# Attention scores built on the array's two 64-row halves, and shifted two query groups later

## The reference, cut to what matters

```
qk  = einsum('bhld,bhrd->bhlr', q, k) / sqrt(16)      # content
qk += einsum('bhld,lrd->bhlr', q, rel_emb[r - l + 511]) # rel: a window that depends on l
att = softmax(qk, axis=-1)
out = einsum('bhlr,bhrd->bhld', att, v)
```

## Time and profile before

| | before |
|---|---|
| median of 3 runs | 6504.95 us (6501.69 to 6511.04) |
| the profiled execution | 6501.09 us |
| its span, first to last instruction | 6499.3 us |
| TensorE busy | 6203.9 us, 95% |
| DVE busy | 5036.1 us, 77% |
| ACT, POOL busy | 48%, 56% |
| TensorE matmuls | 178176 |
| granted TensorE clock | 0.99 of full speed |

### The profile page before, as it was taken

The page is one execution under the profiler, slowest core; times in us unless marked ns, Lnnn a source line. Parts: engine busy times, 40 slices in busy tenths (PEclk is TensorE's granted clock), DMA queues, the critical chain, the costliest instruction groups (busy, mean ns, idle before and its releaser), DMA issues.

```text
span 6499.3 us, 408509 instructions
## 1 busy us (share of the span) xinstructions
PE 6203.9 (95%) x178176; PEld 5783.0 (89%) x178176; DVE 5036.1 (77%) x10289; ACT 3134.0 (48%) x5145; POOL 3640.9 (56%) x4707
## 2 busy tenths in 40 slices
PE   5999999999999999999999999999999999999997
PEld 4999899999999999999999999899999999998997
DVE  3777777777787777777777777777777777777776
ACT  2444444444444444444444444444444444444444
POOL 5555555555565555555555555555555555555555
PEclk8999999999999999999999999999999999999998
DMA  3111121111212112121111211112111121211210
GB/s 86 37 44 50 37 58 37 51 45 35 58 36 59 35 35 61 35 60 33 42 56 35 60 36 48 45 39 58 35 52 43 35 58 38 59 35 33 62 35 27
DMA packets 570089, 296.73 MB, mean 46 GB/s; under 512 B 384176, under 2 KB 534688, under 8 KB 568624
## 3 DMA queue, kind: packets, MB, share of 16 engines
q1 hardware_dynamic: 568624, 272.86, 15.2%
HBM read 184.46 MB, written 88.60 MB: 42 GB/s over the span
## 4 chain that ended last, share of the span: by engine, by line
PE 75%; DVE 15%; issue 6%; DVEq 3%; POOLq 1%; POOL 0%; SPq 0%; ACT 0%; DMA 0%
PE sc L665 19%; PE sc L681 13%; PE sc L660 11%; PE pw L691 11%; DVE r L960 6%; PE pm L672 6%; PE pm L712 4%; PE pw L698 4%; PE pw L712 4%; DVE nm L969 3%; DVE ceq L1008 2%; DVEq L971 2%; DVE y2n L926 1%; DVE dm L983 1%; PE pm L703 1%
## 5 line engine op out<-in xcount | busy, mean ns | idle before, releaser
L960 DVE TRANSPOSE_TENSOR_REDUCE r<-sc 128x32 f32<-128x1024 f32 x2048 | 2547.5, 1244 | 49.2 <-PE sc L665 48.3
L665 PE MATMUL sc<-rm,tw 96*128 96x32 f16 x65536 | 2288.9, 176 | 58.1 <-issue 58.1
L845 ACT ACTIVATE prob<-sc 128x1024 f32<-128x1024 f32 x2048 | 2095.7, 1023 | 237.9 <-PE sc L681 173.7
L665 PEld LDWEIGHTS sc<-rm,tw 96*128 96x128 f16 x65536 | 1976.9, 97 | 64.7 <-issue 64.3
L660 PE MATMUL sc<-qm,ks 96*128 96x64 f16 x32768 | 1635.2, 193 | 29.9 <-DMA ks<-qk_s 15.1
L969 DVE TENSOR_REDUCE nm<-pm 16x32 f16<-16x256 f32 x2048 | 840.5, 410 | 932.2 <-PE pm L672 931.4
L660 PEld LDWEIGHTS sc<-qm,ks 96*128 96x128 f16 x32768 | 1380.8, 98 | 105.7 <-issue 35.2
L681 PE MATMUL sc<-nmm,pick 128*128 128x64 f16 x32768 | 1305.7, 194 | 1.4 <-DVE nmm L972 1.4
L681 PEld LDWEIGHTS sc<-nmm,pick 128*128 128x128 f16 x32768 | 1150.9, 98 | 126.9 <-issue 103.2
L691 PE MATMUL pw<-prob,vs 128*32 128x128 f32 x32768 | 1110.2, 276 | 100.2 <-DVE nm L969 89.9
L691 PEld LDWEIGHTS pw<-prob,vs 128*32 128x32 f32 x32768 | 835.2, 110 | 158.5 <-DVE nm L969 119.8
(11 more groups left out here) (129 smaller groups left out, 5753.9 us busy)
## 6 DMA issues: line engine op xcount, KB each, us to landing
raw<-qk_s SPq DMA_DIRECT2D x774, 64.0 KB, 2.5
tw<-tw_s SPq DMA_DIRECT2D x512, 72.0 KB, 2.0
v_s<-vpad SPq DMA_DIRECT2D x136, 256.0 KB, 3.4
vs<-v_s SPq DMA_DIRECT2D x64, 512.0 KB, 3.7
ks<-qk_s SPq DMA_DIRECT2D x384, 64.0 KB, 2.4
xin<-x SPq DMA_DIRECT2D x138, 128.0 KB, 2.1
qk_s<-qkh SPq DMA_DIRECT2D x272, 64.0 KB, 1.7
qk_s<-qkl SPq DMA_DIRECT2D x272, 64.0 KB, 1.6
```

Of the source, the lines that this page charges most:

```text
L665: last = mm(out3[:, :, 2 * k:2 * k + 2], tw[:, jp, u:u + P], rm[:, i, k, :, :], start=False, stop=False, skip_group_check=True)
L845: A(prob[:, jp % 2, :, :, i * IW:(i + 1) * IW], sc[:, 2 * buf:2 * buf + 2, :].rearrange("p c (h i) -> p c h i", i=IW), ACT.Exp).then_inc(s ...
L960: v.tensor_reduce(r1[:, :], sc[:, 2 * buf:2 * buf + 2, :].rearrange("p c (h i) -> p (c h) i", i=IW), axis=AX.X, op=ALU.max, apply_transpos ...
```

## The change

Content and rel no longer stack two heads or two queries under a mask. The array's rows are used as two halves of 64, of which 48 are filled: the upper half works on key block 0 and the lower on key block 1, each into its own bank. Keys (`ks`) and windows (`tw`) are laid out so, and the queries are copied without a mask in two orders, by head (`qc`) and by query (`qr`). One content matmul is now one head and one key block (32 columns), one rel matmul one query and one key block (16 columns). The shift uses the halves too, with 64 rows. The maxima are transposed with four f16 products on 32-column quarters, and `nmt` is made with four small ones.

A group g now runs on TensorE in this order: transposition of the maxima of group g-2; `wide`; a wait for DVE's reduction; `mixed`; content of g; shift of g-2; rel of g. ACT's copies move by a group or so, and on DVE the spread of group g-2 precedes the maxima of g-1.

```diff
-ROWS = 96
+HALF = 64
+ROWS = HALF + 3 * HD
+LAG = 2
-TWC = 3 * P
+TWC = 2 * P
-        tw_s = nc.dram_tensor("tw_s", (ROWS, NU), f16, kind="Internal").ap()
+        tw_s = nc.dram_tensor("tw_s", (3 * HD, NU), f16, kind="Internal").ap()
-        ks = sb("ks", [ROWS, H // 2, L], f16)
+        ks = sb("ks", [ROWS, H, NJP, P], f16)
-        qm = sb("qm", [ROWS, NI, H, IW], f16)
-        rm = sb("rm", [ROWS, NI, IW // 2, H, 2], f16)
+        qc = sb("qc", [ROWS, NI, H, IW], f16)
+        qr = sb("qr", [ROWS, NI, IW, H], f16)
...
             def load_window(it, jp):
                 u = (TPB - 1) * P - it * P + 2 * P * jp
-                sp.dma_start(tw[:, jp, :], tw_s[:, bass.ds(u, TWC)] ...).then_inc(s_tw[jp], 16)
+                for c in range(2):
+                    v = u + c * P
+                    sp.dma_start(tw[c * HALF:c * HALF + 3 * HD, jp, :], tw_s[:, bass.ds(v, TWC)] ...
...
             def load_keys(b, jp):
-                for s in range(2):
+                for c in range(2):
                     for k, part in enumerate(SPLIT_ST):
-                        j = 2 * P * jp
-                        sp.dma_start(ks[r:r + HD, :, j:j + 2 * P], src[s, :, :, j:j + 2 * P])
+                        j = (2 * jp + c) * P
+                        sp.dma_start(ks[r:r + HD, :, jp, :], src[:, :, j:j + P]).then_inc(s_ks[jp], 16)
...
             def mask(i):
-                g.tensor_tensor(qm[:, i, :, :], src, mask_q[:, :, :], ALU.mult)
-                g.tensor_tensor(rm[...], src..., mask_r[...], ALU.mult).then_inc(s_mask, 1)
+                g.tensor_tensor(qc[:, i, :, :], src, one[0:ROWS, :]..., ALU.mult)
+                g.tensor_copy(qr[:, i, :, :].rearrange("p i h -> p h i"), src).then_inc(s_mask, 1)
...
-            def scores(g, c, buf):
-                for h in range(H // 2):
-                    last = mm(bank[:, 2 * h * IW:(2 * h + 2) * IW], ks[:, h, j:j + P],
-                              qm[:, i, 2 * h:2 * h + 2, :].rearrange("p h i -> p (h i)"), ...
-                for k in range(IW // 2):
-                    u = P - 1 - (i * IW + 2 * k) + c * P
-                    last = mm(out3[:, :, 2 * k:2 * k + 2], tw[:, jp, u:u + P], rm[:, i, k, :, :], ...
+            def content(g, buf):
+                for h in range(H):
+                    for c in range(2):
+                        r = slice(c * HALF, c * HALF + 3 * HD)
+                        mm(sc[:, 2 * buf + c, h * IW:(h + 1) * IW], ks[r, h, jp, :], qc[r, i, h, :], ...
+            def rel(g, buf):
+                for k in range(IW):
+                    u = P - 1 - (i * IW + k)
+                    for c in range(2):
+                        r = slice(c * HALF, c * HALF + 3 * HD)
+                        last = mm(sc[:, 2 * buf + c, :].rearrange("p (h i) -> p h i", i=IW)[:, :, k],
+                                  tw[r, jp, u:u + P], qr[r, i, k, :], ...
             def transpose_max(g_count):
                 for c in range(2):
-                    last = nc.tensor.transpose(p_max[:, c * P:(c + 1) * P], r1[:, c * H:(c + 1) * H], ident[:, :])
+                    for r in (0, HALF):
+                        last = mm(p_max[r:r + 32, c * P:(c + 1) * P], r1[:, c * H:c * H + 32], ident16[:, :], ...
             def shift(buf, g_count):
-                for c in range(2):
-                    for h in range(H // 2):
-                        last = mm(pairs[:, :, h, :], pick[:, h, :], nmm[:, :, :], ...
+                for h in range(H // 2):
+                    for c in range(2):
+                        r = slice(c * HALF, (c + 1) * HALF)
+                        last = mm(pairs[:, :, h, :], pick[r, h, :], nmm[r, :, :], ...
...
             def tile(t, n, att, proj, a, b, ph=None):
+                    if old:
+                        transpose_max(count)
+                    wide(t, n, g, att, proj, a)
+                    if old:
+                        pe.wait_ge(s_nmr, count)
+                    read = mixed(t, g, a, b)
+                    if k == 2 and (a if jp == 0 else att):
+                        for q in range(4):
+                            last = mm(p_nm[32 * q:32 * q + 32, :], nm[...], ident16[:, 0:H], ...
...
-                        scores(g, 0, buffer(ph, g))
+                        content(g, buffer(ph, g))
                     if old:
-                        transpose_max(t * NG + g)
+                        shift(buffer(ph, g - LAG), count)
                     if att:
-                        scores(g, 1, buffer(ph, g)).then_inc(s_scores, 1)
+                        rel(g, buffer(ph, g)).then_inc(s_scores, 1)
```

More of the change, by code:

```diff
@@ L671, in transpose_max @@
                 for c in range(2):
-                    last = nc.tensor.transpose(p_max[:, c * P:(c + 1) * P], r1[:, c * H:(c + 1) * H], ident[:, :])
+                    for r in (0, HALF):
+                        last = mm(p_max[r:r + 32, c * P:(c + 1) * P], r1[:, c * H:c * H + 32], ident16[:, :],
+                                  start=True, stop=True)
                 last.then_inc(s_maxT, 1)
@@ L677, in shift @@
                 pe.wait_ge(s_nm, g_count)
-                for c in range(2):
-                    pairs = sc[:, 2 * buf + c, :].rearrange("p (s h i) -> p s h i", s=2, i=IW)
-                    for h in range(H // 2):
-                        last = mm(pairs[:, :, h, :], pick[:, h, :], nmm[:, :, :],
-                                  start=False, stop=True, skip_group_check=True)
+                for h in range(H // 2):
+                    for c in range(2):
+                        r = slice(c * HALF, (c + 1) * HALF)
+                        pairs = sc[:, 2 * buf + c, :].rearrange("p (s h i) -> p s h i", s=2, i=IW)
+                        last = mm(pairs[:, :, h, :], pick[r, h, :], nmm[r, :, :],
+                                  start=False, stop=(h == H // 2 - 1), skip_group_check=True)
                 last.then_inc(s_shift, 1)
@@ L717, in both, with mixed @@
                 return [(lambda i, c=c: lhs[:, i, c, cols], lambda j, c=c: rhs[:, j, c, :]) for c in range(2)]
[L719 to L728, removed]
+            def mixed(t, g, a, b):
+                if g == 1 and b:
                     pe.wait_ge(s_xn1, t - 1)
@@ L736, in mixed @@
                     return s_hf, t - 1
-                if g == 8 and a:
+                if g == 9 and a:
                     pe.wait_ge(s_o, t)
@@ L797, in tile @@
                     jp, k = divmod(g, NI)
-                    old = a if g == 0 else att
+                    old = a if g < LAG else att
+                    count = t * NG + g - LAG + 1
+                    if read is not None:
+                        pe.wait_ge(*read)
+                    if k == 3 and (a if jp == 0 else att):
+                        pe.wait_ge(s_nmt, t * NJP + jp)
+                    if old:
[6 more added lines that the diff above has]
+                        for q in range(4):
+                            last = mm(p_nm[32 * q:32 * q + 32, :], nm[:, (jp - 1) % 2, 32 * q:32 * q + 32],
+                                      ident16[:, 0:H], start=True, stop=True)
+                        last.then_inc(s_nmtp, 1)
                     if att:
                         if k == 0:
-                            pe.wait_ge(s_tw[jp], t * 16 + 16)
+                            pe.wait_ge(s_tw[jp], t * 32 + 32)
                             pe.wait_ge(s_ks[jp], batch_of(t) * 96 + 96)
@@ L859, in tile @@
                     old = a if jp == 0 else att
-                    if k == 1 and old:
+                    if k == 2 and old:
                         act.wait_ge(s_nmtp, stage + 1)
@@ L864, in tile @@
                             act.wait_ge(s_dm, t)
-                        copy(nmt[:, pj, :], p_n[:, 0:H]).then_inc(s_nmt, 1)
-                    if g == 0 and b:
+                        copy(nmt[:, pj, :], p_nm).then_inc(s_nmt, 1)
+                    if k == 0 and (a if jp < 2 else att):
+                        act.wait_ge(s_ott, stage)
+                        if jp == 2 and a:
+                            act.wait_ge(s_wp, t)
+                        copy(parts[:, (jp - 2) % NJP, :, :],
+                             pw[:, :].rearrange("p (h d) -> p h d", d=32)[:, :, 0:17]).then_inc(s_part, 1)
+                    if g == 1 and b:
                         act.wait_ge(s_x1Tp, t - 1)
```

169 lines of the change are left out of this document (71 added, 98 removed).

## The result

| | before | after |
|---|---|---|
| median | 6503.32 us (4 runs) | 8859.51 us (8856.93 to 8868.53, 4 runs) |
| ratio | | 1.3623, 95% interval 1.3599 to 1.3646 |
| span of the profiled execution | 6499.3 us | 8859.6 us |
| granted TensorE clock | 0.99 | 0.78 |

The change makes the kernel slower by 36%, or 2356 us. The forecast was 9450 us, in a range of 7300 to 10100.

The account below looks back on a forecast made before the run. TensorE's instruction stream bounds the kernel, after the change through the arrival of its blocks: 113 us before the first attention tile, 2285 x 4.08 = 9323 us, some 20 us of tail, 9456 us; range 8800 to 10100, with rivals 7300 to 10100.

Parts of the forecast that it names:

- The blocks as the limit: TensorE's instruction stream: the arrival of its blocks sets the time, 2285 x 4.08 = 9323 us.
- The count: TensorE's matmuls: 103936 on top of 178176; at 124.5 a block, 835 more blocks, 2285 in all.
- The interval: Time between TensorE's instruction blocks: 4.08 us, between 3.85 (densest packets) and 4.37 (when the engine starved).
- rival 3: The instruction fetch is a softer limit: blocks come at 3.3 us under steady demand, 7670 us; chance 0.06.
- The halves overlap: Matmuls on TensorE's two row halves overlap: a group's common work 1577 instead of 1986 ns, -6.5 us a tile.
- Rival 2: The array's halves do not overlap and the blocks keep pace: +2450 us, 8950 us; chance 0.11.
- Changes of mode and waits: TensorE switching ways of using the array: +3.3 us a tile; new waits at most 230 us without a fetch limit.
- rival 1: Instruction blocks keep pace with TensorE, leaving the array's gain: -410 us, 6090 us; chance 0.16.
- Rival 4: TensorE idles for over a third of the time and its clock falls; at half speed 12000 us; chance 0.03.
- The waits on DVE and POOL: TensorE's wait for DVE's reduction and POOL's query copies, beside the fetch: zero, between -10 and +30 us with DMA.
- the signs: 2285 packets, 4.1 us apart; "issue" stalls of 1 to 1.5 us; DVE 53%; rel pairs 25 to 26 ns apart.

Follow-up runs that it names:

- the probe: TensorE's work alone, without the attention layer: the same matmuls on two halves take 14.6 ns each in a short loop, 27.0 ns as straight code.
- rel_one_half: The changed kernel with its rel matmuls reordered, 32 on the upper half, then 32 on the lower, so no two overlap; same instruction count: 9128.45 us.
- rel_half: The changed kernel without every second rel matmul (65536 matmuls fewer, part of the result left out): 7245.76 us.

## Why the prediction was right, step by step

| median us | added in this step | us more |
|---|---|---|
| 6503 | (before) | |
| 6652 | maxima in f16 (on the whole array) | +149 |
| 6882 | order, lag of two, maxima on a quarter, `nmt` in four | +230 |
| 6858 | shift on the halves | -24 |
| 8860 | content and rel split over the halves | +2002 |

**The blocks as the limit: right.** The stalls of the earlier trace rows, two blocks apart, did mean that blocks come one at a time. The probe shows it without anything else, and rel_one_half shows in the kernel that the array's work is not what sets the time: 1395 us more of it cost 269. That the fetch is hidden, as the Trainium skill has it (Runtime: NRT & Kernel Launch, Instruction fetch mechanics), is true for matmuls of 128 columns in the probe, and not for those of 16 on two halves.

**The count: right.** 103936 more matmuls were forecast and found. I divided by 124.5 a block and got 2285 blocks; the division is by 128, and 2261 came. The 124.5 of the earlier trace rows held some other instructions beside.

**The interval: the term that was mis-sized.** I took 4.08 us; it was 3.86 in the mean, at the lower end, and with the 24 blocks too many it makes up the 597 us between the sum's 9456 and the result: 2261 x 0.22 = 498, and 24 x 4.08 = 98. (The 3.86 is worked out from the time itself, so this names the term and proves nothing.) The 4.37 us of the earlier trace rows was not what a starved engine gets: in those 8.7 us the array itself was busy for 8.21 and 8.37 us, so the stretch held mostly work, and was a bad upper end. Alone the interval is 3.45 us, under the 3.85 on which I rested the lower end and closer to rival 3's 3.3; it grows beside heavy transfers. What makes it 3.86 in this kernel, with a mean of 34 GB/s, is only in part known. Other transfers, and blocks whose matmuls take the array longer than their fetch, are candidates. That 4.08 was no worse is partly luck, for the rows that it was taken from did not measure a starved engine.

**The halves overlap: right**, 12.4 ns; it was an inference from `pv`'s quarters. Rival 2 is out. The Trainium skill (TensorEngine Tiling (Array Packing), Instruction Overhead) has some 60 cycles for each matmul; the probe shows that as a cost of one half (26.6 ns), not of the instruction, for two halves take 14.6 ns. Its advice against splitting a small dimension holds here all the same, for the reason of the fetch, which it does not give.

**Changes of mode and waits: too cheap.** I priced the changes at +3.3 us a tile against -6.5. Without the split of content (1.0 of the 6.5), some -5.5 should be left, and the ladder has 6858 - 6503 = 355 us, +2.8 a tile. So the rest costs about 8 us a tile, an estimate: two changes around the shift that the change itself doesn't have (some 3 by the expectation), changes of mode, and the waits of the new order, which I took for nothing behind the fetch and for at most 230 us without it (TensorE's idle time grew by 175). In the result this weighed little, if rel_one_half's fifth holds for it too. Whether rival 1's 6090 us could be reached with the blocks in time is not shown; no run has the split without the blocks.

**Rival 4, the clock: half right.** It fell to 0.78. Idle time, the reason given, isn't needed for it: the probe's loops without a stall ran at 0.53, too. What it costs the kernel no run isolates. Between packets lay 3.78 us in the mean where the clock was full (876 intervals) and 3.95 where it was half (537), which over all blocks would be under 200 us, an estimate from these means.

**The waits on DVE and POOL: small, as forecast.** TensorE waits 77.7 us for DVE's reduction ahead of content and 30.2 for the spread ahead of the shift, where the kernel before had 89.9 us at line 691. POOL's copy in the second order took 2377 ns instead of the masked product's 1180, above the half that I allowed, and stayed hidden but for one wait of 19.2 us.

**Of the signs:** packets (2261 for 2285), stalls named "issue", and pairs of rel matmuls 24.8 ns apart came as written. The packets lie 3.86 us apart, not 4.1, many stalls are shorter than 1 us, and DVE is at 61%, not 53%, as its own work grew from 5036.1 to 5412.9 us.

## What to carry to other kernels

Before splitting one matmul into two smaller ones on parts of the array, count instructions: straight code on TensorE got 128 matmuls with their loads per 3.45 us here (27 ns each), a block took longer with other transfers about (3.86 us in this kernel), and a loop whose body was short enough escaped that. Matmuls of 55.8 ns showed no stall. Where the blocks are late, the faster pairs of matmuls gave nothing in the probe, and fewer instructions gave 1614 us in the kernel (rel_half). And look for stalls with no releaser behind a branch: the number of matmuls between them gives the block, but their distance in time does not give the interval, for the array may have been at work in it.

## What the runs showed of the hardware that was not expected

- TensorE keeps at least 1400 instructions of a loop: the loop of 700 matmuls ran at 14.6 ns each with 5 packets in all over its 9 passes, those of 400, 500 and 600 at 14.2 to 14.4, the one of 900 at 22.7 ns with 33 packets over 8. Straight code gains nothing from that room.
- The granted clock fell without idle time. Loops of 96 matmuls of 48 rows on two halves had 0.53 in the mean with 16 or 32 columns, so they ran mostly at the 1.2 GHz level, and 1.00 (2.4 GHz) with 64; 96 rows had 0.51 with 16 columns and 1.00 with 32. All of these loops kept the engine busy without a pause. The small matmuls suffer little from it: 14.6 ns on the halves at 0.53 in the probe, 12.4 in the run of the kernel after shown above, at 1.00. `pv`'s do: 276 and 418 ns.
- Two small f16 products cost 0.07 us more than the two f32 transpositions of the same shape, and by the starts around them the loss lies just before and just behind them.
- Instruction blocks come later beside heavy transfers: 3.43, 4.68 and 6.35 us a block with 4 (the instructions alone), 182 and 343 GB/s on the queues.
